# Attention value products in groups of eight heads, full-width transposes of the row maxima, and a new order of steps, in a one-core transformer block

## The chip, the core and the metric

The kernel runs on one core of a Trainium2 chip. A core has five engines that work in parallel, each on its own queue of instructions in program order: TensorE (PE in the profile; its weight loads are PEld), VectorE (DVE), ScalarE (ACT), GpSimd (POOL) and SyncE (SP), which here only issues DMAs. They are tied together by semaphores. The metric is the device time of one execution in microseconds (us).

## The reference

One block of a diffusion transformer over 32 batches of 256 tokens with 256 features and 16 heads of 16 features, in float32: modulated self-attention, cross-attention to a context of 256 tokens, and a modulated MLP of width 1024.

```python
c_proj = jax.nn.silu(c) @ W_mod + b_mod
shift_a, scale_a, gate_a, shift_m, scale_m, gate_m = jnp.split(c_proj, 6, axis=-1)
qkv = modulate(_ln(x), shift_a, scale_a) @ W_qkv + b_qkv
attn_w = jax.nn.softmax(jnp.einsum('bhqd,bhkd->bhqk', q, k) * scale, axis=-1)
attn_out = jnp.einsum('bhqk,bhkd->bhqd', attn_w, v)
x = x + gate_a[:, None] * (attn_out @ W_proj + b_proj)
q_c = _ln(x) @ W_qc + b_qc
kv_c = _ln(context) @ W_kvc + b_kvc
...
x = x + c_attn_out @ W_cproj + b_cproj
h = jax.nn.gelu(modulate(_ln(x), shift_m, scale_m) @ W_mlp1 + b_mlp1)
x = x + gate_m[:, None] * (h @ W_mlp2 + b_mlp2)
```

## The kernel before

Every batch goes through some 90 named steps: load, layer norm (`ln`, `norm`), transposes (`t1`, `t2`, `tc`, `t3`), projections (`q`, `k`, `v`, `qc`, `kc`, `vc`, `proj`, `cproj`, `mlp1_0` to `mlp1_3`, `mlp2_0` to `mlp2_3`), and, for self and cross attention each, maxima, exponentials and value products. Projections are float16 matmuls of split operands (a high and a low part, three products in place of one): the steps `x_hi` on ACT and `x_lo` on DVE make the two parts from a PSUM result. One projection (`q`, `k`, `kc`, `mlp1_0`, ...) is 12 matmuls of 128x256 on the full 128x128 array, written as lines 346, 347 and 348 in turn.

Attention of one batch and kind runs over 16 tiles (heads), two at a time:

- `maxima` (L634): four matmuls into `max_ps`, in two row halves of the array; DVE reduces them to row maxima (L986). `max_ps` has one buffer, so the next four matmuls wait for the reduction before.
- `split_...` (DVE) splits the maxima into two float16 parts, `turn_maxima` (PE, steps `m_self` and `m_cross`) transposes them, `m_copy_...` (DVE) copies them out, and DMAs on SP put them under the stacked queries, so that the next step has the maxima subtracted.
- `exps` (L651): four matmuls into `exp_ps`, again one buffer; ACT takes the exponential into the ring `probs` (L791). The next four matmuls wait until ACT has taken those before.
- `values` (L669): for four heads, eight float32 matmuls (16 in the profile, two passes each) with 32 columns of the array for each head, into `o_ps`; ACT copies them out (L799).
- Then SP gathers the sums (`o_gather`), DVE takes their reciprocal (`o_recip`, L996), two DMAs through DRAM spread it (`r_out`, `r_back`), POOL multiplies (`o_norm`, L1092), and `o_hi` (ACT, L804) and `o_lo` (DVE, L999) split the result for the projection.

What sets the order is a timetable. `moment` gives each step of batch n a slot number from `PLAN` (a lag in batches, a half, a slot) less a correction from `AHEAD` for single batches. Every engine walks through the slots in order and, in a slot, through its steps in the order of the code. Slots are not times: an engine goes on as soon as the semaphores let it. Steps of several batches share a slot, so that the work repeats in blocks of 32 slots, one block for each batch. Where this text says "slot s", it means half x 16 + slot of `PLAN`, in such a block. In every even slot PE has one call of `maxima` (slots 0 to 14 self, 16 to 30 cross) and one call of `exps` (cross in slots 6 to 20, self in slots 22 to 30 and 0 to 4). Every second even slot had `values` behind them; the projections fill the rest. The four `mlp1` parts stand together in slot 16, and ACT's GELU for them needs another table of functions than the exponentials, so ACT loads a table before it and another after it. `BANK` assigns the three banks of `dense_ps` to the steps.

Of the kernel before, what the change touches and what calls it, by code (L numbers as in the profile page):

```python
# [27 lines left out]
P = 128  # L28
LN_EPS = 1e-6
TILES = 16  # L30
SHIFT_UNIT = 64.0
# [9 lines left out]
    "o_gather_self": (1, 0, 11), "o_recip_self": (1, 0, 12), "r_out_self": (1, 0, 15), "r_back_self": (1, 1, 1),
    "o_norm_self": (1, 1, 1), "o_hi_self": (1, 1, 3), "o_lo_self": (1, 1, 4), "rows_a": (0, 1, 1),
    "xr": (0, 1, 13), "proj": (1, 1, 6), "x2": (1, 1, 9), "x2_add": (1, 1, 12), "ln2": (1, 1, 13),
    "norm2": (2, 0, 1), "t2": (2, 0, 2), "t2_hi": (2, 0, 2), "t2_lo": (2, 0, 3), "qc": (2, 0, 5),
    "qc_hi": (2, 0, 5), "qc_lo": (2, 0, 6), "stack_qc": (2, 0, 8), "xc": (2, 0, 9), "load_c": (0, 0, 7),
    "lnc": (0, 1, 3), "normc": (0, 1, 8), "tc": (1, 0, 7), "tc_hi": (1, 0, 15), "tc_lo": (1, 1, 0),
    "kc": (1, 1, 3), "kc_hi": (1, 1, 14), "kc_lo": (2, 0, 2), "stack_kc": (2, 0, 7), "vc": (2, 0, 11),
    "vc_hi": (2, 0, 11), "split_cross": (2, 1, 15), "m_cross": (3, 0, 0), "m_copy_cross": (3, 0, 1),
    "o_gather_cross": (3, 1, 11), "o_recip_cross": (3, 1, 12), "r_out_cross": (3, 1, 12),
    "r_back_cross": (3, 1, 14), "o_norm_cross": (4, 0, 3), "o_hi_cross": (4, 0, 3), "o_lo_cross": (4, 0, 4),  # L50
# [1103 lines left out]
```

## Time and profile before

| What | Value |
|---|---|
| Median of 3 runs | 1524.19 us (1521.93 to 1525.54) |
| Profiled execution: its own time | 1521.74 us |
| Profiled execution: span | 1520.0 us |
| Instructions | 39964 |
| Busy: PE, PEld | 1385.0 us, 913.0 us |
| Busy: DVE, ACT, POOL | 1097.0 us, 1100.8 us, 718.9 us |

The span is the time from the first to the last instruction. Busy times are unions of an engine's instruction records. PE's records overlap each other (a matmul's record lasts about 0.27 us where its successor starts 0.11 us later), so PE's busy share hides short waits; the distance between the starts of neighbouring matmuls is the measure to go by.

### The profile page before, as it was taken

How to read it: one execution, taken by the hardware profiler on the slowest of the kernel's cores; microseconds unless marked ns; L12 is line 12 of the kernel's file. 1: busy time of each engine (PE TensorE's matmuls, PEld its weight loads, DVE VectorE, ACT ScalarE, POOL GpSimd, SP SyncE). 2: the span in 40 equal slices, each digit the busy share in tenths (PEclk: the TensorE clock that was granted, in tenths of full speed). 3: DMA queues.
4: the chain of work that ended last, by engine and by line, in shares of the span. 5: the costliest groups of instructions: out<-in, count | busy, mean ns of one | idle time of the engine just before them, and what ended most of it. 6: DMA issues, size and time to landing. Idle time of an engine off the chain costs nothing.

```text
span 1520.0 us, 39964 instructions
## 1 busy us (share of the span) xinstructions
PE 1385.0 (91%) x15090; PEld 913.0 (60%) x15090; DVE 1097.0 (72%) x1965; ACT 1100.8 (72%) x1861; POOL 718.9 (47%) x1005
## 2 busy tenths in 40 slices
PE   3567899999999999999999999999999999988775
PEld 1334566666666666666666666666666666655444
DVE  4648877778777777778877777777887777774511
ACT  3144788777777888777877888887787788877541
POOL 2233354445554554445555455544555545544332
PEclk8689999999999999999999999999999999999987
DMA  5122323333333333233332323323333233221110
GB/s 175 47 82 79 98 89 97 96 95 104 99 93 96 91 95 99 94 99 103 108 95 90 101 91 99 96 94 99 103 106 98 90 100 91 90 77 62 54 44 15
DMA packets 142049, 138.01 MB, mean 91 GB/s; under 512 B 38241, under 2 KB 116226, under 8 KB 141858
## 3 DMA queue, kind: packets, MB, share of 16 engines
q1 hardware_dynamic: 141858, 135.45, 28.6%
q8 instruction: 121, 1.98, 0.6%
q14 instruction: 70, 0.57, 0.1%
HBM read 56.60 MB, written 9.57 MB: 44 GB/s over the span
## 4 chain that ended last, share of the span: by engine, by line
PE 70%; DVE 15%; DMA 4%; issue 3%; POOL 3%; ACT 3%; SPq 1%; DVEq 0%; POOLq 0%; ACTq 0%
PE dense_ps L346 15%; PE dense_ps L347 13%; PE dense_ps L348 13%; PE o_ps L669 11%; PE max_ps L634 9%; DVE mx_cross L986 8%; PE exp_ps L651 6%; PE dense_ps L576 4%; DVE mx_self L986 2%; DMA o_rb_cross<-r_dram_cross 2%; DVE split_k L958 2%; ACT probs L791 1%; DVE ot_self L999 1%; DMA r_dram_cross<-o_r_cross 1%; POOL g_split L1125 1%
## 5 line engine op out<-in xcount | busy, mean ns | idle before, releaser
L791 ACT ACTIVATE probs<-exp_ps 128x1024 f32<-128x1024 f32 x512 | 525.7, 1027 | 189.0 <-PE exp_ps L651 186.6
L986 DVE TENSOR_REDUCE mx_cross<-max_ps 128x4 f32<-128x1024 f32 x256 | 313.4, 1224 | 99.4 <-PE max_ps L634 93.5
L986 DVE TENSOR_REDUCE mx_self<-max_ps 128x4 f32<-128x1024 f32 x256 | 312.5, 1221 | 77.3 <-PE max_ps L634 75.6
L1125 POOL TENSOR_TENSOR g_split<-G,g_split 128x512 f16<-128x512 f32 x128 | 145.7, 1162 | 76.3 <-ACT g_split L780 76.3
L1092 POOL TENSOR_TENSOR o_n_self<-o_n_self,o_rb_self 128x512 f32<-128x512 f32 x32 | 40.6, 1269 | 292.8 <-DMA o_rb_self<-r_dram_self 292.8
L346 PE MATMUL dense_ps<-mlp_hi,g_split 128*128 128x256 f16 x512 | 144.4, 282 | 13.0 <-POOL g_split L1125 13.0
L346 PE MATMUL dense_ps<-xt,mlp_hi 128*128 128x256 f16 x512 | 141.0, 275 | 3.0 <-DVE xt L950 2.8
L347 PE MATMUL dense_ps<-mlp_lo,g_split 128*128 128x256 f16 x512 | 143.4, 280 | 0.0
L348 PE MATMUL dense_ps<-mlp_hi,g_split 128*128 128x256 f16 x512 | 143.4, 280 | 0.0
L347 PE MATMUL dense_ps<-xt,mlp_hi 128*128 128x256 f16 x512 | 140.7, 275 | 0.0
L348 PE MATMUL dense_ps<-xt,mlp_lo 128*128 128x256 f16 x512 | 140.6, 275 | 0.0
L669 PE MATMUL o_ps<-probs,V_self 128*32 128x256 f32 x2048 | 138.6, 388 | 0.0
L669 PE MATMUL o_ps<-probs,V_cross 128*32 128x256 f32 x2048 | 137.0, 385 | 0.2 <-ACT o_sb_cross L799 0.2
L822 ACT ACTIVATE G<-dense_ps,cols_b_all 128x256 f32<-128x256 f32 x256 | 104.0, 470 | 34.8 <-PE dense_ps L348 34.5
L634 PE MATMUL max_ps<-k_stack_cross,q_stack_cross 48*128 48x256 f16 x1024 | 101.0, 276 | 25.8 <-DVE mx_cross L986 20.4
L634 PE MATMUL max_ps<-k_stack_self,q_stack_self 48*128 48x256 f16 x1024 | 101.6, 277 | 20.8 <-DVE mx_self L986 16.2
L1083 POOL TENSOR_SCALAR xn<-X,nm,rs 128x256 f32<-128x256 f32 x192 | 106.4, 562 | 10.5
L1092 POOL TENSOR_TENSOR o_n_cross<-o_n_cross,o_rb_cross 128x512 f32<-128x512 f32 x32 | 40.6, 1270 | 147.9 <-DMA o_rb_cross<-r_dram_cross 147.9
L651 PE MATMUL exp_ps<-q_stack_cross,k_stack_cross 50*128 50x256 f16 x1024 | 98.6, 270 | 12.1 <-ACT probs L791 11.6
L651 PE MATMUL exp_ps<-q_stack_self,k_stack_self 50*128 50x256 f16 x1024 | 100.0, 273 | 9.4 <-ACT probs L791 6.1
L634 PEld LDWEIGHTS max_ps<-k_stack_cross,q_stack_cross 48*128 48x128 f16 x1024 | 29.4, 94 | 94.9 <-DVE mx_cross L986 62.1
L669 PEld LDWEIGHTS o_ps<-probs,V_self 128*32 128x32 f32 x2048 | 53.8, 109 | 49.5 <-issue 27.7
(213 smaller groups left out, 3328.0 us busy)
## 6 DMA issues: line engine op xcount, KB each, us to landing
q_stack_self<-split_q SPq DMA_DIRECT2D x192, 64.0 KB, 2.6
k_stack_self<-split_k SPq DMA_DIRECT2D x192, 64.0 KB, 2.6
k_stack_cross<-split_kc SPq DMA_DIRECT2D x192, 64.0 KB, 2.6
q_stack_cross<-split_qc SPq DMA_DIRECT2D x192, 64.0 KB, 2.6
X<-in_x SPq DMA_DIRECT2D x32, 256.0 KB, 2.7
Ctx<-in_ctx SPq DMA_DIRECT2D x32, 256.0 KB, 3.1
rows_a<-rows_a_dram SPq DMA_DIRECT2D x32, 256.0 KB, 3.4
o_n_self<-o_sb_self SPq DMA_DIRECT2D x64, 128.0 KB, 2.9
```

Of the source, the lines that this page charges most:

```text
L346: eng.matmul(dst, a_hi, b_hi, start=first, stop=False)
L347: eng.matmul(dst, a_hi, b_lo, start=False, stop=False)
L348: return eng.matmul(dst, a_lo, b_hi, start=False, stop=last)
L634: mm = pe.matmul(max_ps[:, ab, qt * T:(qt + 1) * T], q_stack[kind][rows, b.u, p, qt * P:(qt + 1) * P], k_stack[kind][rows, b.u, p], start= ...
L651: mm = pe.matmul(exp_ps[:, ab, kt * T:(kt + 1) * T], k_stack[kind][rows, b.u, p, kt * P:(kt + 1) * P], q_stack[kind][rows, b.u, p], start= ...
L669: mm = pe.matmul(o_ps[32 * j:32 * j + 32, 0, (g % 2) * T:(g % 2 + 1) * T], V[kind][:, b.u, kt, 4 * g + j], probs[:, tile % 8, kt * T:(kt + ...
L791: nc.scalar.activation(probs[:, t % 8:t % 8 + 2], exp_ps[:], ACT.Exp).then_inc(exp_taken[kind], 2)
L822: last = nc.scalar.activation(G[:, f], bank(f"mlp1_{i}")[:, m * T:(m + 1) * T], ACT.Gelu_apprx_tanh, bias=cols_b_all[:, b.n, C + f:C + f + 1])
L986: nc.vector.tensor_reduce(mx[kind][:, :, :, t // 2].rearrange("p q a -> p a q"), max_ps[:].rearrange("p a (q k) -> p a q k", q=2), AX_X, A ...
L1083: last = nc.gpsimd.tensor_scalar(xn[k][:, t], src[:, t], nm[k][:, t:t + 1], rs[k][:, t:t + 1], ALU.add, ALU.mult)
L1092: nc.gpsimd.tensor_tensor(o_n[kind][:], o_n[kind][:], o_rb[kind][:], ALU.mult).then_inc(o_mult[kind], 1)
L1125: nc.gpsimd.tensor_tensor(g_split[:, 1, 2 * i:2 * i + 2], G[:, 2 * i:2 * i + 2], g_split[:, 0, 2 * i:2 * i + 2], ALU.subtract).then_inc(g_ ...
```

## The change

Four things change at once.

1. `values` is called twice for each batch and kind, not four times, with eight heads and 16 matmuls in a call (32 records), into both halves of the `o_ps` bank. It comes in slots 0, 8, 16 and 24. ACT copies 512 columns at once where it copied 256 twice.
2. The ring `probs` grows from 8 to 12 tiles; its start moves with each batch (`ring_start`), and ACT's waits before the exponentials follow.
3. The transposes of the maxima take a window of 128 columns of a widened `mh` (the rest is zeroed once), so that they use the full array, not 32 of its columns.
4. `PLAN`, `BANK` and `AHEAD` are new numbers. `AHEAD` now moves nearly every step of batches 0, 1, 2 and 27 to 31.

```diff
+RING = 12
-    "k": (-1, 1, 2), "k_hi": (-1, 1, 2), "k_lo": (-1, 1, 6), "stack_k": (-1, 1, 6), "v": (-1, 1, 11),
+    "k": (-1, 1, 4), "k_hi": (-1, 1, 4), "k_lo": (-1, 1, 7), "stack_k": (-1, 1, 10), "v": (-1, 1, 11),
...
-                for g in range(4):
+                for g in (1, 3):
                     self.av[moment(f"exp_{kind}", n) + AV_AFTER + 4 * g] = (kind, b, g)
...
+        turns = sorted((moment(f"exp_{k}", n), k, n) for k, n in every)
+        self.ring_start = {turn[1:]: i * TILES % RING for i, turn in enumerate(turns)}
...
-        mh = {k: sb(f"mh_{k}", [P, 2, 2, 2, PAIRS], F16) for k in KINDS}
+        mh_wide = {k: sb(f"mh_{k}", [P, P + 32], F16) for k in KINDS}
+        mh = {k: mh_wide[k][:, 0:64].rearrange("p (q a s r) -> p q a s r", q=2, a=2, s=2) for k in KINDS}
-        probs = sb("probs", [P, 8, 2 * T])
+        probs = sb("probs", [P, RING, 2 * T])
...
-                    mm = pe.transpose(ps[0:32, 0:P].bitcast(F16)[:, qt * P:(qt + 1) * P],
-                                      mh[kind][:, qt].rearrange("p a s r -> p (a s r)"), ident16[:])
+                    mm = pe.transpose(ps[:, 0:P].bitcast(F16)[:, qt * P:(qt + 1) * P],
+                                      mh_wide[kind][:, 32 * qt:32 * qt + P], ident16[:])
...
-                if g >= 1:
-                    pe.wait_ge(o_copied[kind], b.n * 4 + g)
+                if g == 3:
+                    pe.wait_ge(o_copied[kind], b.n * 2 + 1)
                 elif (prev := line.exp_before.get((kind, b.n))):
-                    pe.wait_ge(o_copied[prev[0]], prev[1] * 4 + 4)
-                for kt in range(2):
-                    for j in range(4):
-                        tile = 4 * g + j
...
+                    pe.wait_ge(o_copied[prev[0]], prev[1] * 2 + 2)
+                for half in range(2):
+                    for kt in range(2):
+                        for j in range(4):
+                            tile = 4 * (g - 1 + half) + j
+                            mm = pe.matmul(o_ps[32 * j:32 * j + 32, 0, half * T:(half + 1) * T], V[kind][:, b.u, kt, tile],
+                                           probs[:, (line.ring_start[kind, b.n] + tile) % RING, kt * T:(kt + 1) * T],
...
-                    if t % 4 == 0:
-                        if t >= 8:
-                            act.wait_ge(av_done[kind], b.n * 4 + t // 4 - 1)
-                        elif (prev := line.exp_before.get((kind, b.n))):
-                            act.wait_ge(av_done[prev[0]], prev[1] * 4 + t // 4 + 3)
+                    if t == 12:
+                        act.wait_ge(av_done[kind], b.n * 2 + 1)
+                    elif t == 4 and (prev := line.exp_before.get((kind, b.n))):
+                        act.wait_ge(av_done[prev[0]], prev[1] * 2 + 2)
...
-                    o_sb[kind][:, g % 2, (g // 2) * T:(g // 2 + 1) * T], o_ps[:, 0, cols], ACT.Copy)
+                    nc.scalar.activation(o_sb[kind][:, :, (g // 2) * T:(g // 2 + 1) * T],
+                                         o_ps[:, 0].rearrange("p (h t) -> p h t", h=2), ACT.Copy).then_inc(o_copied[kind], 1)
```

Of the new numbers, these steps matter to the prediction: `k` goes from slot 18 to 20, `tc` from 7 to 15, `t3` from 12 to 15, `mlp2_2` from slot 1 of the next block to 31 (the last slot of this one), `y` from 5 to 3, `o_hi_cross` from 3 to 2.

PE, the place behind the four `mlp1` parts (slots 17 to 20) of a batch in the middle of the run. The rows with `mh_self` are `m_self`, those with `qkv` and `xt` are `k`, those with `kvc` and `xtc` are `kc`. Before:

```order
L348 MATMUL dense_ps<-xt,mlp_lo 128x256
L603 MATMUL dense_ps<-ident,mh_self 32x128 x2
L634 MATMUL max_ps<-k_stack_cross,q_stack_cross 128x256 x4
L651 MATMUL exp_ps<-q_stack_cross,k_stack_cross 128x256 x4
L346 MATMUL dense_ps<-xt,qkv_hi 128x256
...
L346 MATMUL dense_ps<-xtc,kvc_hi 128x256
...
L634 MATMUL max_ps<-k_stack_cross,q_stack_cross 128x256 x4
L651 MATMUL exp_ps<-q_stack_cross,k_stack_cross 128x256 x4
L669 MATMUL o_ps<-probs,V_cross 32x256 x8
```

The same place of the change (its lines are 63 further on):

```order
L411 MATMUL dense_ps<-xt,mlp_lo 128x256
L666 MATMUL dense_ps<-ident,mh_self 128x128 x2
L697 MATMUL max_ps<-k_stack_cross,q_stack_cross 128x256 x4
L714 MATMUL exp_ps<-q_stack_cross,k_stack_cross 128x256 x4
L409 MATMUL dense_ps<-xtc,kvc_hi 128x256
...
L697 MATMUL max_ps<-k_stack_cross,q_stack_cross 128x256 x4
L714 MATMUL exp_ps<-q_stack_cross,k_stack_cross 128x256 x4
L409 MATMUL dense_ps<-xt,qkv_hi 128x256
```

The 12 matmuls of `k` stood between the two calls of `exps` and now stand behind the second one; the values of the first eight heads have gone from here.

DVE, slots 1 to 5 of a block: `mt_cross` is `m_copy_cross`, the reductions are those of `maxima`, `xt` is `t2_lo`, `Y` is `y`, `ot_cross` is `o_lo_cross`. Before:

```order
L981 COPY mt_cross<-dense_ps 32x256
L986 TENSOR_REDUCE mx_self<-max_ps 128x2x2
L958 SCALAR_TENSOR_TENSOR split_kc<-dense_ps,cols_c,split_kc 128x256 x2
L946 TENSOR_TENSOR xt<-dense_ps,xt 128x512
L986 TENSOR_REDUCE mx_self<-max_ps 128x2x2
L999 TENSOR_TENSOR ot_cross<-o_n_cross,ot_cross 128x512
L1035 TENSOR_TENSOR Y<-dense_ps,rows_b 128x512
L986 TENSOR_REDUCE mx_self<-max_ps 128x2x2
```

The same of the change:

```order
L1047 COPY mt_cross<-dense_ps 32x256
L1052 TENSOR_REDUCE mx_self<-max_ps 128x2x2
L1012 TENSOR_TENSOR xt<-dense_ps,xt 128x512
L1101 TENSOR_TENSOR Y<-dense_ps,rows_b 128x512
L1052 TENSOR_REDUCE mx_self<-max_ps 128x2x2
L1065 TENSOR_TENSOR ot_cross<-o_n_cross,ot_cross 128x512
```

`y` has come forward past one reduction (that of slot 4), and `kc_lo` has left for slot 31.

## Rows read from the trace of the kernel before

**Rows 1.** The page: the span.
```profile
span 1520.0 us, 39964 instructions
```

**Rows 2.** Busy time in one stretch: PE, PEld, DVE, ACT, POOL, then the granted clock.
```profile
679.00:1354.00 675.00, 666.49 (x7474) 447.25 (x7472) 533.91 (x936) 541.70 (x908) 349.14 (x492) 1.00 0.31 97
```

**Rows 3.** Line 603 in the same stretch: count, first and last start.
```profile
L603 PE MATMUL dense_ps<-ident,mh_self x34: 219/224/229, 679.0 to 1354.1; 128*32 128x128 f16 x34
```

**Rows 4.** Timeline of PE: start, duration, line; a values call between other calls.
```profile
701.47 1.07 PE L669 MATMUL o_ps<-probs,V_self 128*32 128x256 f32 x16
702.48 0.28 PE L346 MATMUL dense_ps<-xt,qc_hi 128*128 128x256 f16 x1
...
703.89 0.39 PE L634 MATMUL max_ps<-k_stack_self,q_stack_self 48*128 48x256 f16 x4
704.12 0.38 PE L651 MATMUL exp_ps<-q_stack_cross,k_stack_cross 50*128 50x256 f16 x4
704.43 0.28 PE L346 MATMUL dense_ps<-cproj_hi,ot_cross 128*128 128x256 f16 x1
```

**Rows 5.** Timeline of PE behind the mlp1 parts, slots 17 to 24.
```profile
721.05 0.27 PE L347 MATMUL dense_ps<-xt,mlp_hi 128*128 128x256 f16 x1
721.16 0.27 PE L348 MATMUL dense_ps<-xt,mlp_lo 128*128 128x256 f16 x1
721.36 0.28 PE L603 MATMUL dense_ps<-ident,mh_self 128*32 128x128 f16 x2
721.58 0.39 PE L634 MATMUL max_ps<-k_stack_cross,q_stack_cross 48*128 48x256 f16 x4
...
724.85 0.39 PE L634 MATMUL max_ps<-k_stack_cross,q_stack_cross 48*128 48x256 f16 x4
725.08 0.38 PE L651 MATMUL exp_ps<-q_stack_cross,k_stack_cross 50*128 50x256 f16 x4
725.39 1.07 PE L669 MATMUL o_ps<-probs,V_cross 128*32 128x256 f32 x16
726.66 0.39 PE L634 MATMUL max_ps<-k_stack_cross,q_stack_cross 48*128 48x256 f16 x4 [0.20 <-DVE mx_cross L986]
...
729.09 0.39 PE L651 MATMUL exp_ps<-q_stack_self,k_stack_self 50*128 50x256 f16 x4
```

**Rows 6.** Timeline of ACT in that place.
```profile
722.33 1.28 ACT L791 ACT_TABLE_LOAD   x1
723.62 1.02 ACT L791 ACTIVATE probs<-exp_ps 128x1024 f32<-128x1024 f32 x1
...
727.99 1.05 ACT L791 ACTIVATE probs<-exp_ps 128x1024 f32<-128x1024 f32 x1
```

**Rows 7.** Timeline of DVE in that place.
```profile
725.38 1.23 DVE L986 TENSOR_REDUCE mx_cross<-max_ps 128x4 f32<-128x1024 f32 x1 [1.10 <-PE max_ps L634]
726.52 0.73 DVE L999 TENSOR_TENSOR ot_self<-o_n_self,ot_self 128x512 f16<-128x512 f32 x1
727.19 1.23 DVE L986 TENSOR_REDUCE mx_cross<-max_ps 128x4 f32<-128x1024 f32 x1
```

**Rows 8.** Timelines of DVE and ACT: from a reciprocal to the exponential behind the split `ot_cross`.
```profile
734.17 0.35 DVE L996 RECIPROCAL o_r_cross<-o_d_cross 128x32 f32<-128x32 f32 x1
...
744.54 1.01 ACT L791 ACTIVATE probs<-exp_ps 128x1024 f32<-128x1024 f32 x1
```

**Rows 9.** Timeline of PE: a call of transposes, 128x128 float32.
```profile
707.83 0.65 PE L576 MATMUL dense_ps<-ident,xn 128*128 128x128 f32 x4
708.42 0.39 PE L634 MATMUL max_ps<-k_stack_self,q_stack_self 48*128 48x256 f16 x4
```

**Rows 10.** The chain in order of time, near the start: between the first maxima.
```profile
58.50 0.37 PE dense_ps L346
...
61.22 0.57 PE max_ps L634 x4
```

More of the change, by code:

```diff
@@ L41 @@
[L41 to L50, printed above, removed]
[6 rows of a table removed]
+    "load_x": (-2, 1, 14), "ln1": (-1, 0, 1), "norm1": (-1, 0, 1), "t1": (-1, 0, 6), "t1_hi": (-1, 0, 6),
@@ new lines @@
+    "t1_lo": (-1, 0, 10), "q": (-1, 0, 13), "q_hi": (-1, 0, 13), "q_lo": (-1, 0, 14), "stack_q": (-1, 1, 10),
+    "k": (-1, 1, 4), "k_hi": (-1, 1, 4), "k_lo": (-1, 1, 7), "stack_k": (-1, 1, 10), "v": (-1, 1, 11),
+    "v_hi": (-1, 1, 15), "split_self": (0, 1, 0), "m_self": (0, 1, 1), "m_copy_self": (0, 1, 1),
+    "o_gather_self": (1, 0, 12), "o_recip_self": (1, 0, 13), "r_out_self": (1, 0, 15), "r_back_self": (1, 1, 0),
+    "o_norm_self": (1, 1, 2), "o_hi_self": (1, 1, 2), "o_lo_self": (1, 1, 5), "rows_a": (0, 1, 0),
@@ new lines @@
+    "xr": (0, 1, 14), "proj": (1, 1, 7), "x2": (1, 1, 9), "x2_add": (1, 1, 12), "ln2": (1, 1, 13),
+    "norm2": (1, 1, 14), "t2": (2, 0, 0), "t2_hi": (2, 0, 0), "t2_lo": (2, 0, 2), "qc": (2, 0, 4),
+    "qc_hi": (2, 0, 4), "qc_lo": (2, 0, 6), "stack_qc": (2, 0, 7), "xc": (3, 1, 6), "load_c": (0, 0, 1),
+    "lnc": (0, 1, 3), "normc": (0, 1, 15), "tc": (1, 0, 15), "tc_hi": (1, 0, 15), "tc_lo": (1, 0, 15),
+    "kc": (1, 1, 3), "kc_hi": (1, 1, 13), "kc_lo": (1, 1, 15), "stack_kc": (2, 0, 5), "vc": (2, 0, 10),
@@ L57 @@
+    "vc_hi": (2, 0, 13), "split_cross": (3, 0, 0), "m_cross": (3, 0, 0), "m_copy_cross": (3, 0, 2),
+    "o_gather_cross": (3, 1, 10), "o_recip_cross": (3, 1, 12), "r_out_cross": (3, 1, 12),
+    "r_back_cross": (4, 0, 0), "o_norm_cross": (4, 0, 1), "o_hi_cross": (4, 0, 2), "o_lo_cross": (4, 0, 5),
[6 rows of a table added]
 }
 BANK = {
-    "m_self": 0, "m_cross": 2, "qc": 0, "cproj": 2, "tc": 1, "kc": 0, "t3": 0, "mlp1_0": 0, "mlp1_1": 2,
-    "mlp1_2": 1, "mlp1_3": 2, "vc": 0, "t1": 2, "proj": 2, "mlp2": 1, "q": 2, "k": 1, "v": 1, "t2": 2,
+    "m_self": 0, "m_cross": 2, "qc": 2, "cproj": 0, "tc": 1, "kc": 0, "t3": 2, "mlp1_0": 1, "mlp1_1": 2,
@@ L62 @@
+    "mlp1_2": 0, "mlp1_3": 2, "vc": 2, "t1": 1, "proj": 2, "mlp2": 1, "q": 0, "k": 1, "v": 2, "t2": 0,
 }
 AHEAD = {
[L65 to L70 removed]
@@ L847, in _ @@
         def _(dve):
+            for kind in KINDS:
+                nc.vector.memset(mh_wide[kind][:, 64:], 0.0)
             dve.wait_ge(act_set, 1)
```

85 lines of the change are left out of this document (57 added, 28 removed), and 52 rows, old and new, of tables (AHEAD, PLAN).

## The prediction

> **What bounds the kernel now.** I read the page first, then one long stretch of the middle, then the timeline of one block of 32 slots. The span is 1520.0 us [rows 1], the profiled execution took 1521.74 us, and the median of the three runs is 1524.19; I add my changes to the median. In the stretch from 679 to 1354 us PE is busy for 666.49 of 675 us at the full granted clock (1.00), while DVE has 533.91 and ACT 541.70 [rows 2]. So PE bounds the middle, and the question for every edit is what it does to the distance between starts on PE. The stretch holds 34 transposes `m_self`, two for each block, so 17 blocks; from the first to the last start are 675.1 us over 16 blocks [rows 3], 42.19 us for a block. That is the unit of this text: the change acts 28 to 32 times on it.
>
> The reader should then see how little room there is inside a block. PE calls `maxima` every even slot and can't do it again before DVE has reduced the buffer: the reduction starts 0.53 us after the matmuls (724.85 to 725.38), and the next `maxima` 1.28 us after the reduction's start (725.38 to 726.66) [rows 5, 7]. So two calls are at least 1.81 us apart, whatever PE has between them. For `exps` the same loop goes over ACT: the next call starts 1.10 us after the exponential starts (727.99 to 729.09) [rows 5, 6]. An even slot with one projection takes PE 0.23 (`maxima`) + 0.31 (`exps`) + 1.41 (12 matmuls and the change of shape behind them) = 1.95 us [rows 4], 0.14 above the floor. DVE or ACT work of more than that, ahead of the wrong reduction or exponential, is waited for.
>
> **Values in one go.** A values call costs PE 1.01 us to the next start (701.47 to 702.48) [rows 4]. Without it `exps` is followed by the projection after 0.31 us (704.12 to 704.43), and with it by values after the same 0.31 (725.08 to 725.39) [rows 4, 5]: a call that goes away takes its whole 1.01 us with it. What is added to the other call is four rounds of matmuls. Their records run in parallel and the trace doesn't show a round apart; a lower bound of the gain is nothing (the whole cost is matmul time), an upper one the full change of shape at its end. The nearest row for that is 721.16 to 721.36, a 128x256 matmul ahead of another shape: 0.20 us where 721.05 to 721.16 shows 0.11 [rows 5], so 0.09 for a change. Behind values it is a little more, since the last round must drain from 256 rows of float32; I take 0.14. Four calls fewer in a block: 4 x 0.14 = 0.56 us, range 0 to 0.8. ACT saves part of two copies, but ACT is not the bound. The ring of twelve only makes this order possible: the second group's exponentials are four tiles ahead, and ACT's new wait at tile 12 is for values that PE has called two slots before. I cost it at nothing; the cover is one even slot of PE work, 1.95 us.
>
> **Full-width transposes.** `m_self` stands between a projection and `maxima`. Entering it costs 0.20 where it would cost 0.11 without a change of shape [rows 5]: 0.09 us a block. Leaving it for `maxima` is a change in either form. `m_cross` follows values, of the 32-column shape as it was itself: there the change moves from behind it to ahead of it, gain 0 (bounds 0 and 0.09).
>
> **`k` behind the second `exps`.** This is the largest term, and it speaks against the change. At the end of the `mlp1` parts ACT still has the last GELU, then loads the table of the exponential (722.33, 1.28 us), and only then takes the exponential of tile 12 (723.62) [rows 6]. PE's next `exps` may start 1.10 us later, at 724.72. It did so at 725.08, 3.72 us after `m_self` at 721.36 [rows 5], because `k` and `kc` filled the time: 0.36 us of slack. Now only `kc` stands there. PE would come to that call at: last `mlp1` start 721.16 + 0.11, `m_self` and on to `maxima` 0.22 (721.36 to 721.58), then 0.23, 0.31, 1.41, and 0.23 [rows 4, 5] = 723.67. ACT's dates hang on the last GELU and don't move. PE waits for 724.72 - 723.67 = 1.05 us in every block, and `k` is still to be done behind it. (It swallows the 0.09 of `m_self`, which is why that is counted once, above.) Queued behind the waiting `exps` are `k` and the `maxima` of slot 22; DVE gets ahead in the meantime, which helps it in slots 22 and 24 only. I take 1.05; bounds 0.9 and 1.1.
>
> The Trainium skill, page "ScalarE: Activation LUTs", section "What ACT_TABLE_LOAD costs", states about 1283 ns for the load and some 1380 ns more of drain for each switch of the set. The row has the first part (1.28 us) and not the second: the exponential starts 0.01 us behind the load's end. By the rows this term is 1.05 us; by the page's whole figure, were the drain to come on top, it would be 2.43.
>
> **Other slots that get tight.** Three more, each read off the new order.
> - Slot 14 now has only `tc` and `t3`, two calls of transposes of about 0.59 us [rows 9]: 0.23 + 0.31 + 0.50 (no change of shape behind the first) + 0.59 = 1.63, 0.18 below the floor of 1.81. I take 0.15; bounds 0 and 0.18.
> - `y` now stands ahead of the reduction of slot 4. With M for the start of that `maxima`: the reduction of slot 2 began at M - 1.95 + 0.53 and takes 1.14 to the next DVE start (725.38 to 726.52 [rows 7]), `t2_lo` and `y` 0.67 each (726.52 to 727.19, a like operation [rows 7]), so the reduction begins at M + 1.06, not M + 0.53, and the next `maxima` at M + 2.34 where PE would be there at M + 1.95. Since `t2_lo` reads 512 columns in one instruction I allow 0.1 less: cost 0.3, bounds 0 and 0.4.
> - `o_hi_cross` is a slot earlier, ahead of the exponential of slot 4. From the reciprocal (734.17) to the exponential behind that split (744.54) are 10.37 us, mostly two DMAs through DRAM [rows 8], plus 1.10 to the next `exps`: 11.47. PE's own way from slot 30 (24 matmuls) over 0 (values), 2 and 4 to the `exps` of slot 6 is about 3.3 + 3.1 + 1.95 + 2.25 + 0.23 = 10.8. Cost between 0 and 0.6; I take 0.3, since the reciprocal's own start may come earlier by as much.
>
> What goes away: the block of before had waits too, in slots with values alone. 725.39 to 726.66 is 1.27 where values take 1.01 and a change of 0.11, and `exps` at 729.09 was some 0.14 late [rows 5]: 0.3 us a block that the new order may not have.
>
> **Start and end.** In the first block DVE and PE alternate on `maxima`, and 12 matmuls of the next batch's `q` stood between two of them (58.50 to 61.22, 2.7 us [rows 10]); the new `AHEAD` puts them behind all eight. I take -3 us. For the last batches nearly all steps move by a few slots, in both directions; no row prices that, and I take 0, within -8 and +8.
>
> **Sum.** A block: -0.56 - 0.09 + 1.05 + 0.15 + 0.3 + 0.3 - 0.3 = +0.85 us. The waits need `mlp1` parts of one batch beside cross attention of the next, which is so in 28 blocks or so: +23.8 us. With the start: +20.8, less 2 us for the values calls of the 4 blocks outside: about +19. 1524.19 + 19 = 1543 us, 1.2% slower.
>
> **Rivals.**
> - *PE stays the bound and the change does what it says.* The `exps` behind `kc` finds its buffer free, and the small waits don't come. Then -0.65 - 0.3 in a block is at most -30, without the 0.3 -21, and with the start -24: 1500 us. What speaks for it: PE's busy share of 99% [rows 2], and that the gains are of PE's own time. Against it: 723.62 + 1.10 is read from rows, and the new order has nothing between. It decides the sign if the wait is under 0.3 us. Chance 0.22.
> - *The large wait comes, the small ones don't, or the gain of values is 0.2 a call.* 1.05 - 0.65 - 0.3 is +0.1 a block, with the start 0 us: 1517 to 1530, around 1524. Chance 0.15.
> - *More waits than I have found.* The reciprocal's chain late by its full 0.6, POOL late for `norm1` (it now stands behind `o_norm_cross`), GELU late for `mlp1_3` since ACT copies values of eight heads ahead of its table load: +0.6 a block, +17 us: 1560. Chance 0.12.
> - *The drain of the page does come into the wait.* 1.38 us more in 28 blocks, +39: 1582. The row behind the load speaks against it [rows 6]. Chance 0.01. (This is the rule of the Trainium skill's page "ScalarE: Activation LUTs" as above.)
>
> **How the numbers follow.** My forecast, slower by 0.4 to 2.2% (1530 to 1558), has a chance of 0.5; the rivals the rest. To leave out no more than 2 in 10 the range must go into the first rival: 1506 to 1562. The likeliest case's own range is 1530 to 1558. A measurement of this kernel tells 0.2% (3 us) from no change: faster 0.24, same 0.08, slower 0.68.
>
> **What would show it.** In the profile after: values calls of about 1.87 us to the next start, half as many (right: below 1.9; wrong: 2.0). `m_self` 0.11 behind the last `mlp1` matmul. In the list of waits PE or its weight loads waiting for ACT's `probs` at the `exps` behind `kc`, about 1 us each, some 28 us in all, where before such waits were few. A block of 43.0 us by the starts of `m_self` (41.3 if the first rival holds). PE's busy time in the middle below 98%. I am wrong if that `exps` starts within 0.3 us of where PE comes to it, or if the end of the run, from the last `m_self` on, is more than 10 us shorter.

## The result, and the profile after

Measured beside the kernel before on the same chip, the change takes 1571.09 us (median of 4 runs, 1567.54 to 1576.54) against 1524.62 us (4 runs, 1521.93 to 1525.54): ratio 1.0303, 95% interval 1.028 to 1.0326. It is slower, by 46 us where +19 was forecast; the time lies above the range (1506 to 1562). The sign was right, the size was not.

The page after, the span and the busy times:

```profile
span 1565.7 us, 39710 instructions
PE 1378.6 (88%) x15090; PEld 928.0 (59%) x15090; DVE 1103.4 (70%) x1967; ACT 1096.6 (70%) x1733; POOL 721.1 (46%) x1005
```

The span grew by 45.7 us [rows 1]. To see where, I cut it at the starts of `m_self`, one pair for each block. These are the rows of line 666 (after) in three windows, and of line 603 (before) in the same three:

```profile
L666 PE MATMUL dense_ps<-ident,mh_self x10: 217/229/314, 71.6 to 233.2; 128*128 128x128 f16 x10
L666 PE MATMUL dense_ps<-ident,mh_self x36: 219/219/219, 447.2 to 1178.5; 128*128 128x128 f16 x36
L666 PE MATMUL dense_ps<-ident,mh_self x12: 219/219/230, 1178.5 to 1400.2; 128*128 128x128 f16 x12
```
```profile
L603 PE MATMUL dense_ps<-ident,mh_self x10: 217/219/314, 71.2 to 211.8; 128*32 128x128 f16 x10
L603 PE MATMUL dense_ps<-ident,mh_self x36: 219/224/230, 425.3 to 1143.2; 128*32 128x128 f16 x36
L603 PE MATMUL dense_ps<-ident,mh_self x12: 219/224/229, 1143.1 to 1354.1; 128*32 128x128 f16 x12
```

Now the busy times of the same stretches, after and then before (columns as in [rows 2]):

```profile
71.60:233.20 161.60, 121.70 (x1153) 69.59 (x1154) 101.36 (x175) 84.50 (x127) 43.25 (x75) 0.84 0.24 73
447.10:1178.40 731.30, 699.37 (x7959) 484.14 (x7957) 569.40 (x1003) 575.67 (x901) 375.44 (x528) 1.00 0.31 96
1178.40:1400.20 221.80, 206.42 (x2336) 140.59 (x2334) 165.81 (x291) 168.54 (x263) 108.60 (x151) 1.00 0.31 92
```
```profile
71.20:211.80 140.60, 106.00 (x1130) 62.58 (x1130) 98.78 (x173) 81.35 (x130) 49.16 (x77) 0.92 0.28 85
425.20:1143.00 717.80, 710.20 (x7958) 476.61 (x7956) 569.86 (x1003) 576.88 (x969) 372.65 (x528) 1.00 0.31 97
1143.00:1354.00 211.00, 207.18 (x2326) 138.69 (x2324) 165.37 (x287) 168.38 (x281) 108.33 (x151) 1.00 0.31 96
```

Each stretch tells another story.

- *17 middle blocks*: +13.5 us, 0.79 a block. PE is busy 10.83 us less (0.64 a block) and idle 31.9 instead of 7.6 us (1.43 more a block).
- *First four blocks*: +21.0 us with about as many instructions. PE is busy 15.7 us more, at a granted clock of 0.84 instead of 0.92, and idle 5.3 us more.
- *Last five blocks*: +10.8 us, all idle time of PE (15.4 instead of 3.8 us).
- The head, the five blocks between the first and the second stretch and the tail differ by half a microsecond or less each. For those five blocks the forecast had 5 x 0.85 = 4.3 us; the kernel before took 213.4 us for them where five of its later blocks take 211.

The waits of PE in the middle stretch (engine, operation, releaser: us in total, times, longest), after and then before:

```profile
PE exp_ps L714 <- ACT probs L855: 22.5, 23, 1.8
PE max_ps L697 <- DVE mx_self L1052: 6.7, 22, 1.0
```
```profile
PE max_ps L634 <- DVE mx_cross L986: 4.0, 18, 0.6
PE exp_ps L651 <- ACT probs L791: 1.4, 2, 1.0
```

The place of the largest term, PE after (start, duration; compare [rows 5]):

```profile
705.23 0.27 PE L666 MATMUL dense_ps<-ident,mh_self 128*128 128x128 f16 x2
705.44 0.39 PE L697 MATMUL max_ps<-k_stack_cross,q_stack_cross 48*128 48x256 f16 x4
...
707.40 0.39 PE L697 MATMUL max_ps<-k_stack_cross,q_stack_cross 48*128 48x256 f16 x4
708.66 0.39 PE L714 MATMUL exp_ps<-q_stack_cross,k_stack_cross 50*128 50x256 f16 x4 [0.87 <-ACT probs L855]
708.98 0.28 PE L409 MATMUL dense_ps<-xt,qkv_hi 128*128 128x256 f16 x1
...
712.90 1.93 PE L733 MATMUL o_ps<-probs,V_cross 128*32 128x256 f32 x32
714.77 0.39 PE L697 MATMUL max_ps<-k_stack_cross,q_stack_cross 48*128 48x256 f16 x4
```

and ACT there (compare [rows 6]):

```profile
706.28 1.28 ACT L855 ACT_TABLE_LOAD   x1
707.58 1.02 ACT L855 ACTIVATE probs<-exp_ps 128x1024 f32<-128x1024 f32 x1
```

`exps` comes 1.26 us behind its `maxima` and not 0.23, so it is held for 1.03 us; it starts 1.08 us after the exponential of tile 12. A values call of eight heads takes 1.87 us (712.90 to 714.77) where two old ones took 2.02 [rows 4]. `m_self` stands 0.11 us behind the last `mlp1` matmul, as forecast.

A surprise is that every fourth block of the middle stretch is some 1.5 us longer than its neighbours: 43.8 to 44.3 us, the others 42.4 to 43.1 (the waits of up to 1.8 us above are in these). In one such block, after:

```profile
632.31 0.33 SPq L518 DMA_DIRECT2D r_dram_cross<-o_r_cross  x1
...
635.37 1.24 SPq L526 DMA_DIRECT2D o_rb_cross<-r_dram_cross  x2
...
641.57 1.26 POOL L1158 TENSOR_TENSOR o_n_cross<-o_n_cross,o_rb_cross 128x512 f32<-128x512 f32 x1 [3.56 <-DMA o_rb_cross<-r_dram_cross]
...
642.87 0.63 ACT L868 ACTIVATE ot_cross<-o_n_cross 128x512 f16<-128x512 f32 x1 [2.83 <-POOL o_n_cross L1158]
```
```profile
642.39 0.39 PE L697 MATMUL max_ps<-k_stack_self,q_stack_self 48*128 48x256 f16 x4 [0.15 <-DVE mx_self L1052]
644.56 0.39 PE L714 MATMUL exp_ps<-q_stack_cross,k_stack_cross 50*128 50x256 f16 x4 [1.77 <-ACT probs L855]
```

In the block ahead of it the two DMAs stood 1.81 us apart:

```profile
589.58 0.32 SPq L518 DMA_DIRECT2D r_dram_cross<-o_r_cross  x1
...
591.39 0.62 SPq L526 DMA_DIRECT2D o_rb_cross<-r_dram_cross  x1
```

The second DMA waits for the landing of the first: 3.06 us here, 1.81 there. (In the five long blocks this distance is 2.78 to 3.27 us, in the other twelve 1.41 to 2.30.) Then `o_n_cross` is late on POOL, ACT holds the exponential of slot 4 behind the split `ot_cross`, and PE the `exps` of slot 6.

### The profile page after: what moved, and what is told of

It is laid out like the page before. It is cut to its first block, busy times and chain, and to the rows that moved or that the text cites. A ratio compares the mean times of both kernels' runs of the same rounds, so it can differ in the third digit from the quotient of the medians.

```text
span 1565.7 us, 39710 instructions
## 1 busy us (share of the span) xinstructions
PE 1378.6 (88%) x15090; PEld 928.0 (59%) x15090; DVE 1103.4 (70%) x1967; ACT 1096.6 (70%) x1733; POOL 721.1 (46%) x1005
## 4 chain that ended last, share of the span: by engine, by line
PE 46%; SPq 16%; DMA 10%; DVE 10%; ACT 7%; issue 6%; POOL 4%; POOLq 0%; DVEq 0%; ACTq 0%
SPq L494 13%; PE o_ps L733 10%; PE dense_ps L409 9%; PE dense_ps L411 8%; PE dense_ps L410 8%; PE max_ps L697 5%; DVE mx_self L1052 4%; PE exp_ps L714 4%; DMA o_d_self<-o_sb_self 3%; ACT probs L855 3%; DMA o_rb_cross<-r_dram_cross 3%; DMA o_d_cross<-o_sb_cross 2%; SPq L501 2%; ACT L855 2%; DMA r_dram_cross<-o_r_cross 1%
## 5 line engine op out<-in xcount | busy, mean ns | idle before, releaser
L733 PE MATMUL o_ps<-probs,V_self 128*32 128x256 f32 x2048 | 129.4, 395 | 0.0
L733 PE MATMUL o_ps<-probs,V_cross 128*32 128x256 f32 x2048 | 125.8, 387 | 0.6 <-ACT probs L855 0.6
L1149 POOL TENSOR_SCALAR xn<-X,nm,rs 128x256 f32<-128x256 f32 x192 | 110.8, 584 | 10.5
L733 PEld LDWEIGHTS o_ps<-probs,V_self 128*32 128x32 f32 x2048 | 61.7, 113 | 50.0 <-issue 19.0
L733 PEld LDWEIGHTS o_ps<-probs,V_cross 128*32 128x32 f32 x2048 | 60.6, 111 | 48.9 <-issue 15.7
L1141 POOL TENSOR_SCALAR ve<-mv 128x2 f32<-128x2 f32 x96 | 19.7, 205 | 150.9 <-DVE mv L1006 148.4
```

What stands on the lines that cost most here:

```text
L733: mm = pe.matmul(o_ps[32 * j:32 * j + 32, 0, half * T:(half + 1) * T], V[kind][:, b.u, kt, tile], probs[:, (line.ring_start[kind, b.n] + t ...
L1149: last = nc.gpsimd.tensor_scalar(xn[k][:, t], src[:, t], nm[k][:, t:t + 1], rs[k][:, t:t + 1], ALU.add, ALU.mult)
```

## The experiments

Each was timed in rounds against the kernel before on the same chip (its medians lie between 1522 and 1525 us). Blocks and stretches are those of the cuts above. Of tables only the rows that differ are shown; where a step is moved in `PLAN`, the other rows stay. A yardstick for the middle stretch: in the change, e4, e5, e6 and e10 to e13 PE has the same calls there in the same order (but for 16 of 7956 matmuls in e5 and e6), and the stretch takes 728.3 to 736.2 us, 42.8 to 43.3 a block. Differences smaller than that say little.

**e1, the code on the old plan.** after.py with the `PLAN`, `BANK` and `AHEAD` of before.

```diff
-PLAN, BANK, AHEAD of the change
+PLAN, BANK, AHEAD of before
```

> Values of eight heads, ring of twelve and full-width transposes, but every number of PLAN, BANK and AHEAD as before. Theory A (the new order is what costs): the code alone gains its 0.65 us a block less the waits that it makes in the slots that lose their values call: slot 20 has then nothing between maxima and the next maxima (0.54 us of PE work against a floor of 1.81 us, 1.27 us of waiting) and slot 12 only t3 (1.13 against 1.81, 0.7 us), so about +1 us a block over before, 1545 to 1560 us. Rival B (the two parts add up independently and the gain is there): 0.65 us a block less than before, about 1504 us. The start and the end of the run as before: 20 us less than in the changed kernel in the first four blocks, 10 us less in the last five.

Measured 1581.60 us, ratio 1.0394 (1.034 to 1.0448). Windows and waits, middle stretch:

```profile
440.10:1186.00 745.90, 702.69 (x7957) 483.68 (x7956) 568.50 (x1003) 574.22 (x901) 373.31 (x529) 1.00 0.31 94
```
```profile
PE max_ps L652 <- DVE mx_cross L1007: 21.7, 20, 1.2
...
```

PE is busy 7.5 us less than before, and idle 43.2 us. The largest wait is 1.2 us once a block: slot 20 has lost its values, PE has only `exps` behind `maxima` and comes back to the next `maxima` while DVE has not reduced the buffer. The code alone needs a new order; on the old one it costs 1.66 us a block. Theory A named this wait, but had only 1 us a block, and it expected the start as before, where the first four blocks take 149.2 us in place of 140.6: its 1545 to 1560 us was missed as well as B's 1504.

**e2, the new plan alone.** before.py with the three tables of the change.

```diff
-PLAN, BANK, AHEAD of before
+PLAN, BANK, AHEAD of the change
```

> The code of before (values of four heads, ring of eight, transposes of 32 columns) with the new PLAN, BANK and AHEAD. Theory A (start and end tables and the wait behind kc cost, whatever the code): the middle block is that of the changed kernel (42.4 us) plus 0.65 for the code, less 0.2 for short waits that the extra values calls fill: 42.9 us; the first four blocks stay some 20 us longer than before; 1575 to 1590 us in all. Rival B (the ring and the values calls cause the waits): below 1550 us. The exps behind kc still starts about 1 us late under A.

Measured 1606.98 us, 1.0539 (1.0498 to 1.058), 44.37 us a block in the middle stretch, above both theories (A had 42.9 a block and 1575 to 1590 us). PE waits there 17.4 us for `probs`, 9.3 for `mx_self` and 9.1 for `xt`. The first four blocks take 157.7 us, with the old values calls: the loss of the start is for the most part there without calls of eight heads. Either half alone is worse than both: e1 43.88, e2 44.37, the change 43.02, before 42.22. Their costs don't add.

**e3, `k` back in slot 18.** (The rows of `AHEAD` for `k` and `k_hi` are reduced by 2, so that batches 0 to 2 and 27 to 31 keep their places.)

```diff
-    "k": (-1, 1, 4), "k_hi": (-1, 1, 4),
+    "k": (-1, 1, 2), "k_hi": (-1, 1, 2),
```

> The changed kernel with k and k_hi back in slot 18, together with kc (batches 0 to 2 and 27 to 31 keep their places). Theory A, the one of the prediction (that wait is the cost of having moved k, and goes with it): 1.03 us less in 23 blocks, 24 us less, about 1547 us. Rival B (the wait only changes its name): slot 20 then has no matmul between exps and the next maxima, DVE's floor of 1.81 us is waited for there, 1.27 us in place of 1.03, and the time is the same or up to 6 us more, 1570 to 1578 us.

Measured 1577.95 us, 1.0352 (1.0287 to 1.0418). Waits of PE in the middle stretch:

```profile
PE max_ps L710 <- DVE mx_cross L1065: 20.4, 17, 1.2
...
PE exp_ps L727 <- ACT probs L868: 5.3, 5, 1.6
```

The wait for ACT at that `exps` is gone and another of 1.2 us stands in each of the 17 blocks, at the `maxima` behind slot 20, which is now empty (43.10 us a block, 43.02 before the edit). Rival B held. So the term of the forecast was real, but its cause is wider than "`k` stands behind `exps`": with the values of slot 20 gone there is work for one of the slots 18 and 20, and either place is waited for.

**e4, e5, e6, without rows of `AHEAD`**: of batches 0 to 2, of 27 to 31, and all.

```diff
-AHEAD = {0: {...}, 1: {...}, 2: {...}, 27: {...}, ... 31: {...}}
+AHEAD = {27: {...}, ... 31: {...}}          # e4
+AHEAD = {0: {...}, 1: {...}, 2: {...}}      # e5
+AHEAD = {}                                  # e6
```

> The changed kernel without the AHEAD rows of batches 0, 1 and 2, which then follow PLAN. Theory A (the 21 us lost in the first four blocks come from those rows, which set the DMAs of SP and the DVE steps in another order): the first four blocks near the 140 us of before, 10 to 20 us less in all, about 1555 us. Rival B (they come from the new PLAN itself or from waiting behind eight-head values while PE's clock is low): within 5 us of the changed kernel, or slower since nothing is pulled ahead.

> The changed kernel without the AHEAD rows of batches 27 to 31. Theory A (the last five blocks, 221.7 us where five middle blocks would be 213, lose 8 us to those rows): the five blocks take about 213 us; what follows the last m_self, 165.6 us, gets longer since nothing is pulled ahead any more, by an unknown amount; 1560 to 1580 us in all. Rival B: the five blocks stay above 219 us, because the plan itself or the data of the last batches is the cause.

> The changed kernel with AHEAD empty: the base for the kernel that fills the slots again. Start as in the kernel without the start rows (first four blocks 149 us), end as in the one without the end rows; about 1560 us, and a middle block of 42.6 us.

e4 took 1561.83 us (1.0249, 1.0204 to 1.0294), e5 1576.74 (1.0354, 1.0319 to 1.0388), e6 1569.27 (1.0307, 1.0279 to 1.0334). In e4 the first four blocks take 149.4 us instead of 161.6:

```profile
73.70:223.10 149.40, 115.13 (x1140) 67.61 (x1141) 99.38 (x173) 81.20 (x121) 45.40 (x74) 0.84 0.26 80
```

PE is busy 6.6 us less than in the change and idle 5.6 us less. Head, tail and the other blocks of the profiled execution are 11.6 us longer in sum (the tail alone 4.5), so its span is that of the change. (It was the longest of e4's four executions, and the change's was its shortest.) The medians are 9.3 us apart, and those of the two other pairs that differ by the start rows 7.5 (e5, e6) and 6.4 (e12, e13). The cut at the fourth block is steady all the same: with the start rows, or most of them, it is 157.6 to 162.5 us in six kernels (the change, e2, e3, e5, e10, e12), without them 149.4, 150.7 and 151.2 (e4, e6, e13). Theory A of e4, near 140, was half right. The rows of the end do two things: without them (e5) the last five blocks are 8.3 us shorter, 213.4 us as Theory A of e5 had it, and the tail is 16.1 us longer. So they cause most of what the last five blocks lost, and are worth having. e6 was expected at 1560 us; it has both, the shorter start and the longer tail. (`AHEAD` has 59 to 80 of the 96 steps of each of these batches.)

**e7, even slots refilled** (without `AHEAD`): a projection for each slot that had only `maxima` and `exps`.

```diff
-"k": (-1, 1, 4), "v": (-1, 1, 11), "v_hi": (-1, 1, 15), "mlp2_0": (4, 1, 13), "mlp2_1": (4, 1, 15), "y": (5, 0, 3)
+"k": (-1, 1, 2), "v": (-1, 1, 4), "v_hi": (-1, 1, 6), "mlp2_0": (4, 1, 11), "mlp2_1": (4, 1, 13), "y": (5, 0, 5)
...
+# k_hi as k, y_add as y, xc from (3, 1, 6) to (3, 1, 10)
```

> The changed kernel with AHEAD empty and seven steps moved so that PE has both cover for the table load and work in every even slot: k and k_hi to slot 18 beside kc, v to 20 and v_hi to 22 (from 27 and 31), mlp2_0 from 29 to 27, mlp2_1 from 31 to 29, xc from 22 to 26 and y, y_add to 5 to clear POOL and DVE for it. Theory A (PE is the bound wherever each even slot has 1.8 us of work and the second exps behind mlp1 is covered): the wait of 1.03 and those of the thin slots go, a middle block of 41.3 to 41.7 us, 30 us less than the same without the moves. Rival B (other queues, g_lo on POOL ahead of mlp2_0 or stacked k on SP, take the place of the wait): 42.2 us or more, less than 12 us gained.

Measured 1694.28 us, 1.1138 (1.1089 to 1.1186), 47.0 us a block. One wait of PE explains most of it:

```profile
PE dense_ps L330 <- ACT V_self L755: 56.9, 17, 3.4
```

The projection in slot 22 uses the buffer that `v` filled in slot 20, and ACT copies it out only behind an exponential and three GELU splits. (The middle stretch of e6, which differs from e7 in the slots alone, has 43.1 us a block.)

**e9, refilled with `v_hi` in slot 21**, `normc` and `load_c` in the slots of the kernel before, and `xc` in another one (its diff is against e7).

```diff
-"v_hi": (-1, 1, 6), "xc": (3, 1, 10), "normc": (0, 1, 15), "load_c": (0, 0, 1)
+"v_hi": (-1, 1, 5), "xc": (2, 0, 11), "normc": (0, 1, 8), "load_c": (0, 0, 7)
```

> The change without any AHEAD rows, and the even slots refilled as in the last attempt (k and k_hi in slot 18, v in slot 20, mlp2_0 in 27, mlp2_1 in 29, y in slot 5), but with the copy V_self of v_hi one step later than v in slot 21, xc back in slot 11 of the lap, normc and load_c as they were before the change, so that neither the projection in slot 22 nor SP has to wait. Theory A (the price of the middle is the empty even slots, and the last refill failed only by v_hi and the transfers): the wait of 3.4 us in slot 22 goes, the block falls from 47.3 to under 42.3 us, below the 42.63 of the same tables with the slots as the change has them, and the time is under 1562 us. Rival B (a slot that is filled takes its work from another, and copies that come earlier or later on ACT and DVE are waited for elsewhere): the wait in slot 22 goes, but the block stays at 42.8 us or more and the time at 1575 us or more.

Measured 1604.28 us, 1.0536 (1.0506 to 1.0566), 44.02 us a block:

```profile
PE exp_ps L635 <- ACT probs L776: 15.1, 17, 1.5
PE dense_ps L330 <- ACT V_self L755: 10.8, 17, 0.6
PE max_ps L618 <- DVE mx_cross L973: 9.3, 17, 0.8
PE dense_ps L330 <- POOL g_split L1112: 6.5, 17, 0.4
```

The wait of 3.4 us fell to 0.6, and others stand in each block: the three above and one of `maxima` for `mx_self` (6.1 us, 17 times). Rival B again: a slot that is filled has its inputs and its buffer to wait for. Whether an order exists in which nothing waits (PE's busy time would allow 41.2 us a block: 699.9 us in 17) was not found.

**e8, full-width transposes alone**, on the code and plan of before.

```diff
-mm = pe.transpose(ps[0:32, ...], mh[kind][:, qt] ..., ident16[:])
+mm = pe.transpose(ps[:, ...], mh_wide[kind][:, 32 * qt:32 * qt + P], ident16[:])
```

> The kernel of before with the full-width transposes of the maxima alone. Theory A: m_self starts 0.11 in place of 0.20 us behind the last mlp1 matmul, and since the exps two slots on have 0.36 us of slack the 0.09 us a block stay gained: 2 to 3 us in all, a middle block of 42.0. m_cross gains nothing. Rival B (nothing is gained since the table load sets the date of the exps): block of 42.1, no difference.

Measured 1518.47 us (10 runs), ratio 0.9982 (0.9964 to 1.0). It is the only kernel here that is not slower than before, and its gain of 2.7 us (by the ratio) is no more than its interval. Theory A had 2 to 3 us, but a middle block of 42.0, where the profile has 42.3. PE's busy time in the middle stretch did not fall (711.29 us in 17 blocks, 710.20 before), but in kernels with the same calls it differs by up to 5 us from one execution to another, so it can't show 0.09 us a block. The starts of PE can: in each of the 17 blocks of e8 `m_self` stands 0.11 us behind the matmul ahead of it and `maxima` 0.21 behind `m_self` (0.20 and 0.22 before), and `m_cross` 0.31 behind the values and 0.12 ahead of what follows (0.20 and 0.21 before). That is 0.10 saved at `m_self` and 0.02 lost at `m_cross`, close to the 0.09 and 0 of the prediction.

**e10, e11, which rows of the start**: the change with the rows of batches 0 to 2 cut for the front steps (e10), or for four steps of the way back (e11).

```diff
-0: {"load_x": 61, "ln1": 62, ..., "v_hi": 17, ...}     # e10: load_x to v_hi, batches 0 to 2
-0: {"stack_qc": -2, "o_gather_self": 3, "r_out_self": 2, "r_back_self": 3, ...}   # e11
```

> The change, with the AHEAD rows of batches 0 to 2 cut for the steps from load_x to v_hi (loads, t1, q, k, v, their splits and stacks: what is pulled ahead by 20 to 60 moments); the rest of those rows stays. The first four blocks took 161.6 us in the change and 149.4 without any of its start rows. Theory A (it is the front steps, lumped early, which leave PE thin afterwards and let its clock fall): about 150 us in the first four blocks, time near 1562. Rival B (it is the way back of the attention output, late behind stack_qc on SP's queue): the first four blocks stay at 159 us or more and the projection of batch 0 in the fourth block still starts after more than 2 us of waiting for ot_self.

> The change, with the AHEAD rows of batches 0 to 2 cut for stack_qc, o_gather_self, r_out_self and r_back_self alone (the transfers on SP's queue and the way of the row sums over DRAM). Rival B of the previous kernel (the transfers of the way back are late): the first four blocks fall from 161.6 us to about 150, the wait of the projection for ot_self in the fourth block goes, and the time is near 1562. Theory A (front steps): they stay at 159 us or more and the time at 1568 or more.

e10 took 1579.23 us (1.0376, 1.0341 to 1.0411), its first four blocks 162.5 us, with the longest wait of a projection for `ot_self` at 2.7 us: not the front steps alone. e11 took 1582.09 us (1.0388, 1.0342 to 1.0434), its first four blocks 170.6 us:

```profile
PE dense_ps L420 <- DVE ot_self L1076: 7.3, 2, 6.8
```

In the change this wait was 3.0 us in total, and in e4 there was none. The rows that e11 leaves out had put `r_out_self` and `r_back_self` one to four slots earlier; without them the way of the row sums is later still. e10 speaks against the front steps as the cause and e11 against these four; which of the start rows carry the loss stays open.

**e12, `o_hi_cross` behind the exponential of slot 4.**

```diff
-    "o_hi_cross": (4, 0, 2),
+    "o_hi_cross": (4, 0, 4),
```

> The change with one number altered: o_hi_cross at (4, 0, 4) instead of (4, 0, 2), so that ACT splits ot_cross behind the exponential of slot 4 and not ahead of it. Theory A (about every fourth block the landing of r_dram_cross takes 3 us instead of 1.8, o_n_cross is then late, ACT holds the exponential of slot 4 behind the split, and PE waits 1.8 us at the exps of slot 6): the long blocks of 43.8 to 44.3 us fall to about 42.5, the middle 22 blocks from 945.3 us to 937 to 939, the time to 1561 to 1566 us. Rival B (the lateness passes to the projection cproj in slot 6 or to DVE's half of the split, and is waited for there): the long blocks stay above 43.5 us and the time at 1569 us or more.

Measured 1579.71 us, 1.0382 (1.0354 to 1.041). Waits of PE in the middle stretch:

```profile
PE exp_ps L727 <- ACT probs L868: 14.8, 17, 0.9
PE dense_ps L422 <- DVE ot_cross L1078: 8.3, 17, 1.1
```

The cause was placed rightly and the gain was not there. `exps` waits 17 times, 0.87 us each, which is the wait of tile 12 alone; the long ones are gone (22.5 us to 14.8). The 7.7 us stand one step further on, 8.3 us at `cproj` of slot 6, which needs `ot_cross`, now in every block: Rival B. The middle stretch is the same (731.6 us), but the kernel is 8.6 us slower than the change, clear of both intervals. In the profile that is at the end: the last five blocks and the tail are 12.8 us longer, and PE waits there 10.1 us for `ot_cross` where the change waits 1.8. The edit moves the split of the last batches too, whose rows of `AHEAD` stay as they were.

**e13, the same without the rows of the start.**

> The same edit of o_hi_cross, and the AHEAD rows of batches 0 to 2 left out. If the two losses are separate they add: -9 us of the start rows and -7 of the long blocks, 1553 to 1557 us, still 2% above the kernel before. If the start rows only shift where the same DMA lateness is met, the gain is that of the larger one, 1561 us or more.

Measured 1573.33 us, 1.0334 (1.0305 to 1.0362). That is 11.5 us more than e4 and outside what was expected (1553 to 1557, or 1561 and more with a gain). First four blocks 151.2 us about as in e4, the middle stretch 736.2 us where e4 had 734.5, the last five blocks 227.8 where it had 222.2. What leaving out the start rows gives stands by itself, and the edit of e12 costs again.

## Why the prediction was wrong, step by step

**The middle was right.** Forecast +0.85 us a block, measured +0.79 in the 17 blocks of the middle stretch (0.6 to 1.1 by the spread of the kernels with the same calls there, so an agreement this close is in part luck). Term by term:

- *Values and transposes*: -0.65 forecast, PE's busy time fell by 10.83 / 17 = 0.64. By the timeline the values gave 0.15 a call, four times, and the transposes 0.10 at `m_self` less 0.02 at `m_cross`: 0.68.
- *The wait of tile 12*: 1.05 forecast, 1.03 by the starts of the calls (0.87 as the list of waits counts it, which leaves out what hides behind weight loads and the queue). e3 says what the forecast did not: it can't be taken away by putting `k` back.
- *`o_hi_cross`*: 0.3 forecast, 7.7 / 17 = 0.45 measured by e12. It is not 0.3 in each block but nothing in most and up to 1.8 us in every fourth. The order of steps that I read for it was not its cause alone: before, too, the split stood ahead of an exponential, and landings as late were there too (the next DMA up to 3.07 us behind; the block with 2.89 us took 42.2 us, that with 3.07 took 43.5). In the change each of the five at 2.78 us and more stands in a long block. So what is new seems to be that the chain through DRAM has less time to spare; no run here changes that time alone.
- *Slot 14 and `y`*: 0.15 + 0.3 forecast, 6.7 / 17 = 0.39 as waits of `maxima` for `mx_self`.
- *Old waits gone*: 0.3 forecast, 5.4 / 17 = 0.32 in the two rows of before.
- *Idle time in all*: 1.5 forecast, 1.43 measured.

**The step that failed is the one called "Start and end": "I take -3 us", and for the last batches "I take 0, within -8 and +8".** The head, in which the order stood that the -3 us were read from, takes as long as before (71.6 and 71.2 us). The first four blocks cost +21.0 us, and the last five +10.8, where 5 x 0.85 = 4.3 was in the sum: 24 and 6.5 us are what is missing. (The five blocks ahead of the middle stretch took some 4 us less than forecast.) I had priced one order of instructions on PE (12 matmuls of `q` between two `maxima`) and not the rows of `AHEAD`, nor the granted clock.

*The last five blocks.* e5 shows the step: the rows of batches 27 to 31 put 8.3 us into these blocks, of which I took none, and take 16.1 us out of the tail.

*The first four blocks* fall into two halves that lose for different reasons. The windows of the halves in the change, then in e4:

```profile
71.60:139.00 67.40, 47.38 (x417) 25.56 (x418) 36.44 (x68) 29.51 (x45) 14.42 (x28) 0.79 0.23 69
139.00:233.20 94.20, 74.32 (x737) 44.03 (x738) 64.92 (x108) 55.00 (x82) 28.84 (x47) 0.87 0.24 76
```
```profile
73.70:143.40 69.70, 49.77 (x404) 25.88 (x405) 35.35 (x66) 29.18 (x43) 17.91 (x29) 0.72 0.23 71
143.40:223.10 79.70, 65.36 (x736) 41.74 (x737) 64.03 (x108) 52.02 (x78) 27.48 (x45) 0.96 0.28 89
```

The same halves in other kernels, in us, with the granted clock:

| Kernel | Values of | Start rows | Blocks 1, 2 | Blocks 3, 4 |
|---|---|---|---|---|
| before | 4 heads | old | 60.6 (0.88) | 79.9 (0.96) |
| e8 | 4 heads | old | 60.6 (0.86) | 80.5 (0.92) |
| e1 | 8 heads | old | 68.9 (0.79) | 80.4 (1.00) |
| e4 | 8 heads | none | 69.7 (0.72) | 79.7 (0.96) |
| e2 | 4 heads | new | 66.3 (0.84) | 91.4 (0.93) |
| change | 8 heads | new | 67.4 (0.79) | 94.2 (0.87) |
| e5 | 8 heads | new | 67.4 (0.79) | 91.6 (0.91) |
| e12 | 8 heads | new | 63.1 (0.86) | 94.5 (0.87) |

- *Blocks 3 and 4* lose 12 to 15 us in the kernels of the table with the new start rows, with either form of values, and take about as long as before without them. In the change, against e4, PE is busy 9.0 us more for the same number of matmuls, at a lower granted clock, and idle 5.5 us more; in the pair e5 and e6 it is 2.7 us busy and 7.9 idle, so the two shares are not steady. Of the idle time 3.0 us are waits for `ot_self`, the way back of the attention output; e2 waits 4.7 us for it there, e4 not at all.
- *Blocks 1 and 2* lose 8 us with values of eight heads on the old tables (e1; e8 rules the transposes out, the ring of twelve came with the values). 6.5 of them are in the first block, where PE is busy 21.62 in place of 16.11 us for the same number of matmuls, at a clock of 0.65 in place of 0.81. On the new tables the form of values makes little difference (e2 and the change).

So the granted clock is part of both. In the first block PE's calls stand far apart, and the eight-head call can fall where only half the clock is granted. The first two values calls after the first `m_self` in the change, and one of before at the same stage:

```profile
87.61 3.06 PE L733 MATMUL o_ps<-probs,V_self 128*32 128x256 f32 x32
94.77 1.93 PE L733 MATMUL o_ps<-probs,V_self 128*32 128x256 f32 x32
```
```profile
82.09 1.07 PE L669 MATMUL o_ps<-probs,V_self 128*32 128x256 f32 x16
```

In the first four blocks of the change 5 of 11 values calls take 2.8 to 3.6 us in place of 1.93, and 100 of 360 projection matmuls last longer than 0.34 us (0.42 at the half clock, 0.27 at the full one); before, 41 of 336. That is most of the 15.7 us of more busy time; the instructions are 2% more. But the clock is not set by the order alone: in the first three blocks the change, e5 and e12 run the same program, and the first block takes 34.8, 35.1 and 30.7 us, at clocks of 0.70, 0.74 and 0.89.

Not settled: which of the start rows carry the 12 us (neither those cut in e10 nor those in e11 do alone), how much of it would stay if the clock did not fall (nothing here holds the clock up without moving work), and whether the calls of eight heads lower the clock or were met by a low one.

**The rivals.** "PE stays the bound" fell with the first waits. "The drain of the page does come into the wait" would have given 1582, nearer to the measured time than my forecast, but not by its mechanism: `exps` was held 1.03 us and not 2.4, and the exponential of tile 12 starts 0.02 us behind the end of the table load (706.28 + 1.28 to 707.58). The Trainium skill, page "ScalarE: Activation LUTs", section "What ACT_TABLE_LOAD costs", has about 1283 ns for the load, with which this trace agrees, and 1380 ns of drain, which it does not show here. "More waits than I have found" (1560) had the right sign, for a reason that was not among its three: the start and the end. (Of the three, only the lateness of the chain through DRAM was seen, and it was in the forecast at 0.3.)

## What to carry to other kernels

A call that is merged leaves two slots behind, one fuller and one emptier. Where each slot has a floor set by another engine (here 1.81 us for DVE's reduction), PE time that is saved in an empty slot is waited away (1.2 us once a block in e1), so compare each slot with the floor before and after and not the sum of PE's time. Filling the slot again brings its inputs and its buffer with it, as e3, e7 and e9 show.

Cut the span at a repeated instruction into start, middle and end, and price each from its own rows: here the middle was forecast to within 0.1 us a block, and two thirds of the loss were in nine blocks that I had given a guess of -3 and 0.
